# Two transformer layers in one kernel: the second attention's weights, first projections and constant rows moved into the experts' last batch

## The chip, the core and the metric

The kernel runs on one core of a Trainium2 chip. A core has five engines with queues of their own: PE (TensorE, matrix products into PSUM), ACT (ScalarE), DVE (VectorE), POOL (GpSimd) and SP (SyncE, which here issues nearly all DMAs). They are tied together by semaphores alone. The metric is the device time of one execution in microseconds (us), lower is better: 1503.14 us before the change, the median of three runs (1500.72 to 1504.99).

## The reference

Input `x` is 4 batches x 512 tokens x 256 features, all in float32. Two pre-norm layers:

```python
x = x + L0_attn(layernorm(x))   # 16 heads of 128, 8 kv heads, RMS norm, RoPE, window 128
x = x + L0_ffn(layernorm(x))    # 16 experts of 176, top 6 by softmax gate, and a shared one of 352
x = x + L1_attn(layernorm(x))   # below
x = x + L1_ffn(layernorm(x))    # ternary-quantized weights, 256 -> 1024 -> 256, exact gelu

def L1_attn(x):                 # 16 heads of 16
    q, k, v = (x @ W for W in (Wq, Wk, Wv))       # each split in heads
    p = softmax(q @ k.T * 0.25)
    return (p @ v) @ Wo + bo
```

## The kernel before

Nothing is tiled over cores; each layer part runs over the four batches, and a batch's 512 tokens are one tile of 512 columns. Products that need float32 precision are made of three passes in a faster format: every operand is split in a high and a low part (`_hi`, `_lo`), the high by a copy on ACT, the low by a subtraction on DVE or POOL, and `split_product` multiplies low x high, high x low, high x high. The order of the work on each engine is written out by hand, in functions of the same name for each engine: `attention_step` (first attention), `expert_step`, `pair_step` (second attention), `mlp_step`. Each step waits for semaphore counts that are worked out from the step's number. Middle batches run in hardware loops (`Fori`), the first and last are written out.

**Experts.** `expert_step(b, j, new, old)`: batch b, slice j of 25 slices of 128 hidden features. PE makes gate and up products of slice j (12 matmuls), ACT applies silu (L1168), DVE multiplies (L834), PE spreads the routing weight (`combine`, L1459), DVE multiplies by it (L844), ACT copies the high part (L1148), DVE subtracts the low (L850), and PE multiplies by the down weights (`down`, two steps behind). `new` says that there is a batch b in this step, `old` that batch b-1 still has work. After slice 24 come, with `b = 4` and `new` false, four steps in which only the last slices of batch 3 are finished, turned (L1447) and added to `x_res` (L818, semaphore `y_added`). The layer norm of the next layer part's first batch is made inside the last expert batch: `xnT` is ready in step 25.

**Between experts and second attention.** SP waits until all of `y_added` is there, then loads the second attention's weights (`wqk1`, `wv1`, `wo1`), a 1 MB tile of constants for `v1` (`c_vones`), the bias and the last layer's weights (2 MB). ACT and DVE split `wqk1`, PE projects tile 0 of q and of k (a tile is 8 heads of 16, 128 rows; `project_tile`), ACT and DVE split them into `qk1`.

**Second attention.** Heads of 16 rows are small for a 128-row array. So a head's q and k are stacked: high, high, low of q over high, low, high of k, 48 rows, and a row of ones in k beside the negated row maximum in q, 64 rows per head, two heads (a pair) in 128. The stacking changes partitions, and is done by DMA through a scratch tensor in DRAM: `keep_copies(b, tile)` writes six copies (L377), `stack_pair(b, n)` reads pair n back (L389) into rings of four, `qst` and `kst`. The constant rows of these rings are set once, on POOL and DVE (L506 to L508, L945). `pair_step(b, n, new, old)` is pair n of batch b, eight places i in it: scores for the maximum (L1583), reduced on DVE (L909), maxima turned (L1608) and added to q (`qsm`), scores again transposed (L1596), exponentials on ACT (L1223, tile pT), products with v (L1622, ring of two pairs), result copied by ACT (oT, L1255, at place i = 5 of each even pair), turned by PE (L1636, at i = 6) and divided on DVE. Spread over these places are the remaining projections: tile 1 of q at (n, i) = (0, 5), of k at (1, 3), the values in halves at (2, 5) and (3, 0), tile 0 of the next batch at (4, 5) and (5, 3), and the turns of the next batch's normed input. Their result goes through PSUM bank 0; ACT copies the high part and the raw value, POOL subtracts (`low_tile`, L525), `raw_kept` and `raw_used` count this.

SP issues its DMAs strictly in the order of its program. In batch b that is: copies of tile 0, pairs 0 to 3, copies of tile 1, pairs 4 to 7; `stack_pair` waits until the pair four before has been used, and at n = 0 and 4 until the copies have landed.

Of the kernel before, what the change touches and what calls it, by code (L numbers as in the profile page):

```python
# [13 lines left out]
F32 = mybir.dt.float32  # L14
# [7 lines left out]
P = 128  # L22
# [30 lines left out]
VW = 32  # L53
# [5 lines left out]
STACK_ROWS = 3 * HD1  # L59
STACKED = 2 * 2 * 16  # L60
# [3 lines left out]
RAW_USES, FIRST_USES, LAST_USES = 8, 6, 6  # L64
# [8 lines left out]
def build(nc, dram, out):  # L73
    with ExitStack() as ctx:
# [84 lines left out]

        wqk1 = [sb(f"wqk1_{part}", [P, KT, 2 * D], F32R, part_c) for part in ("hi", "lo")]  # L160
        wv1 = [sb(f"wv1_{part}", [P, KT, D], F32R, part_c) for part in ("hi", "lo")]

        vzero = sb("vzero", [P, STACK_RING * SEQ], where=part_c)
        pT1 = sb("pT1", [P, 2, 4, TT, SEQ], where=part_c)
        wo1 = sb("wo1", [P, KT, D], where=part_c)
        bo1 = sb("bo1", [P, D], where=part_c)
        stack = sb("stack", [P, 4], where=part_c)
        v1 = sb("v1", [P, TT, HEADS1 * VW], where=part_c)
        qk1 = [sb(f"qk1_{part}", [P, 2, 2, SEQ], F32R, part_c) for part in ("hi", "lo")]
        qst = sb("qst", [P, STACK_RING, SEQ], F32R, part_c)  # L170
        kst = sb("kst", [P, STACK_RING, SEQ], F32R, part_c)
        qsm = sb("qsm", [P, 2, SEQ], F32R, part_c)
        nm1 = sb("nm1", [P, 2, TT, P], where=part_c)

        early = pT1[:, 1].rearrange("p h c f -> p h (c f)")
        wqk1_in, wv1_in = early[:, 0, 0:KT * 2 * D], early[:, 1, 0:KT * D]
        oT1 = sb("oT1", [P, 2, SEQ], where=part_c)
        oinv = sb("oinv", [P, 2, TT, 4], where=part_c)
        otok = sb("otok", [P, TT, D], where=part_c)
        oTn = sb("oTn", [P, KT, SEQ], where=part_c)  # L180

        wm1 = sb("wm1", [P, KT, DFF], where=part_c)
        wm2 = sb("wm2", [P, HT, D], where=part_c)
        ones = sb("ones", [P, P], where=part_c)
# [1659 lines left out]
```

## Time and profile before

| | us |
|---|---|
| median of 3 runs | 1503.14 |
| profiled execution | 1504.41 |
| its span | 1502.7 |
| PE busy | 1395.5 (93%) |
| DVE busy | 1084.1 (72%) |
| ACT busy | 731.6 (49%) |
| POOL busy | 471.9 (31%) |

The first attention takes the span up to about 690 us, the experts up to 1089, the second attention up to about 1415, the last layer part the rest. The profile's mean granted clock of PE is 0.957 of full speed; full is 2.4 GHz, the other level, 1.2 GHz, shows as 0.50. In timelines the length of a matmul is that of one from issue to end; back to back they overlap.

### The profile page before, as it was taken

The numbers are of one execution on the slowest core, as the hardware profiler recorded it, in microseconds if no ns is written. First come the engines' busy times: TensorE is split into PE (matmuls) and PEld (weight loads), VectorE is DVE, ScalarE is ACT, GpSimd is POOL, SyncE is SP. The second block draws the span as 40 slices with busy tenths as digits, with TensorE's granted clock in tenths as the row PEclk, the third lists the DMA queues.
The fourth block names the chain that finished last, engine by engine and source line by source line (L and its number), as shares of the span: only waits on it lengthen the run. The fifth ranks groups of instructions, "written<-read, shape, count | busy, mean of one in ns | idle before, by whom it ended". The sixth has DMA issues, their size and how long they took to land.

```text
span 1502.7 us, 24489 instructions
## 1 busy us (share of the span) xinstructions
PE 1395.5 (93%) x7518; PEld 1058.9 (70%) x7518; DVE 1084.1 (72%) x2508; ACT 731.6 (49%) x1885; POOL 471.9 (31%) x727
## 2 busy tenths in 40 slices
PE   4799999999999998899999999999849899999898
PEld 3689889888998897677777777777624344444476
DVE  6999999899999995676555555455436776677454
ACT  4555565556556553444322322322216566666575
POOL 5766657666765663000000000000023031312110
PEclk9899999999999999899999999999957899999999
DMA  5200000000000000322000000000062222232001
GB/s 181 71 2 2 2 2 1 3 1 2 1 1 1 2 1 17 116 86 63 1 1 1 0 0 0 0 0 0 0 203 71 84 85 91 89 91 77 1 15 43
DMA packets 30941, 52.80 MB, mean 35 GB/s; under 512 B 4496, under 2 KB 12688, under 8 KB 30448
## 3 DMA queue, kind: packets, MB, share of 16 engines
q1 hardware_dynamic: 30432, 50.76, 10.9%
q8 instruction: 53, 0.87, 0.3%
q0 software_dynamic: 400, 0.71, 0.3%
q14 instruction: 56, 0.46, 0.1%
HBM read 37.49 MB, written 14.68 MB: 35 GB/s over the span
## 4 chain that ended last, share of the span: by engine, by line
PE 70%; DVE 13%; POOL 5%; issue 5%; ACT 4%; DMA 2%; SPq 1%; DVEq 0%; ACTq 0%; POOLq 0%
PE ps L1309 13%; PE ps L1311 13%; PE ps L1310 13%; PE ps L1583 5%; PE ps L1622 4%; PE ps L1395 4%; PE ps L1353 4%; POOL rope L462 2%; DVE qkn L705 2%; DVE ssum L716 2%; PE ps L1708 2%; POOL rms L460 2%; PE ps L1459 2%; PE ps L1381 1%; PE ps L1730 1%
## 5 line engine op out<-in xcount | busy, mean ns | idle before, releaser
L909 DVE TENSOR_REDUCE nm<-ps 128x1 f32<-128x512 f32 x256 | 166.2, 685 | 92.9 <-PE ps L1583 92.4
L1309 PE MATMUL ps<-xnT_lo,w1moe_hi 128*128 128x512 f32 x400 | 178.2, 445 | 2.0 <-DVE w2moe_lo L867 1.8
L1223 ACT ACTIVATE pT<-ps 128x512 f32<-128x512 f32 x256 | 142.5, 598 | 73.6 <-PE ps L1596 72.4
L1310 PE MATMUL ps<-xnT_hi,w1moe_lo 128*128 128x512 f32 x400 | 161.6, 404 | 0.0
L1311 PE MATMUL ps<-xnT_hi,w1moe_hi 128*128 128x512 f32 x400 | 160.5, 401 | 0.0
L421 POOL TENSOR_TENSOR ln_rs<-ln_ve,minus_half 128x4 f32<-128x4 f32 x12 | 13.6, 1131 | 466.3 <-DVE ln_ve L579 466.3
L1148 ACT ACTIVATE moe_act_hi<-sg 128x512 fp32r<-128x512 f32 x100 | 63.4, 634 | 190.3 <-DVE sg L844 190.3
L834 DVE TENSOR_TENSOR sg<-ps,sg 128x512 f32<-128x512 f32 x100 | 69.0, 690 | 97.4 <-ACT sg L1168 97.3
L462 POOL TENSOR_TENSOR rope<-rope 128x384 f32<-128x384 f32 x128 | 132.6, 1036 | 0.0
L1309 PE MATMUL ps<-wqkv_lo,xnT_hi 128*128 128x512 f32 x256 | 126.9, 496 | 6.1 <-issue 3.2
L1583 PE MATMUL ps<-kst,qst 64*128 64x512 f32 x256 | 106.9, 495 | 16.5 <-DMA kst<-copies 14.5
L1395 PE MATMUL ps<-qkT 128*128 128x128 f32 x896 | 121.9, 276 | 0.0
L680 DVE TENSOR_TENSOR yT<-yT,rsums 128x256 f32<-128x256 f32 x128 | 116.1, 907 | 3.2
L1596 PE MATMUL ps<-qsm,kst 64*128 64x512 f32 x256 | 110.9, 495 | 6.4 <-ACT pT L1223 6.4
L850 DVE TENSOR_TENSOR moe_act_lo<-sg,moe_act_hi 128x512 fp32r<-128x512 f32 x100 | 69.2, 692 | 65.4 <-ACT moe_act_hi L1148 65.3
L460 POOL TENSOR_TENSOR rms<-msq,minus_half 128x3 f32<-128x3 f32 x128 | 110.4, 863 | 10.0
L1108 ACT ACTIVATE yT<-ps,nmax 128x128 f32<-128x128 f32 x256 | 92.4, 373 | 39.6 <-DVE nmax L696 39.3
L1395 PEld LDWEIGHTS ps<-qkT 128*128 128x128 f32 x896 | 111.1, 193 | 0.5
L1168 ACT ACTIVATE sg<-ps 128x512 f32<-128x512 f32 x100 | 59.8, 598 | 101.6 <-PE ps L1311 101.5
L1583 PEld LDWEIGHTS ps<-kst,qst 64*128 64x128 f32 x256 | 45.1, 204 | 89.1 <-DVE nm L909 52.0
L1068 ACT ACTIVATE probT<-ps 128x256 f32<-128x256 f32 x128 | 49.2, 384 | 111.8 <-PE ps L1353 56.7
L1353 PE MATMUL ps<-parted,v 128*128 128x256 f32 x384 | 99.3, 381 | 3.8 <-POOL parted L448 1.9
(213 smaller groups left out, 3701.6 us busy)
## 6 DMA issues: line engine op xcount, KB each, us to landing
copies<-qk_hi SPq DMA_DIRECT2D x32, 256.0 KB
yT<-in_w1moe SPq DMA_DIRECT2D x25, 256.0 KB, 2.6
qst<-copies SPq DMA_DIRECT2D x64, 96.0 KB, 2.2
kst<-copies SPq DMA_DIRECT2D x64, 96.0 KB, 2.2
x_res<-in_wqkv SPq DMA_DIRECT2D x8, 512.0 KB, 4.8
copies<-qk_lo SPq DMA_DIRECT2D x16, 256.0 KB
w_in<-in_w2moe SPq DMA_DIRECT2D x25, 128.0 KB, 2.7
x_res<-in_wo SPq DMA_DIRECT2D x4, 512.0 KB, 3.9
```

Of the source, the lines that this page charges most:

```text
L460: nc.gpsimd.tensor_tensor(rms[:, s, :], msq[:, s, :], minus_half[:, 0:3], ALU.pow).then_inc(rms_ready, 1)
L462: nc.gpsimd.tensor_tensor(rope1[:, s, :], rope1[:, s, :], rope2[:, s, :], ALU.add).then_inc(rotated, 1)
L680: V.tensor_tensor(prob[:, m % PROB_RING], prob[:, m % PROB_RING], rsums[:, s, :].unsqueeze(2).to_broadcast((P, 2, P)), ALU.mult).then_inc( ...
L909: V.tensor_reduce(nm1[:, n % 2, t, col:col + 1], ps[:, 1 + s1_slot(p), :], AX.X, ALU.max, negate=True).then_inc(s1_max, 1)
L1223: A(pT1[:, u % 2, 2 * (m % 2) + h, c, :], ps[:, 4 + e % 2, :], ACT.Exp, scale=SCALE1).then_inc(p1_ready, 1)
L1309: MM(out, left[0], right[1], start=first, stop=False)
L1310: MM(out, left[1], right[0], start=False, stop=False)
L1311: return MM(out, left[0], right[0], start=False, stop=last)
L1353: ins = MM(ps[:, 6, 0:2 * P], v0[:, (m if part else m - GROUPS) % V_RING, :], parted[:, r, part].rearrange("p h f -> p (h f)"), start=part ...
L1395: ins = MM(bank[:, h, part, :], qkT[:, m % K_RING, h, :], qkT[:, (m if part else m - GROUPS) % K_RING, 2, :], start=not alone(m) and h == ...
L1583: MM(ps[:, 1 + s1_slot(p), :], qst[rows, n % STACK_RING, t * P:(t + 1) * P], kst[rows, n % STACK_RING, :], start=True, stop=True).then_inc ...
L1596: MM(ps[:, 4 + e % 2, :], kst[rows, m % STACK_RING, c * P:(c + 1) * P], qsm[rows, m % 2, :], start=True, stop=True).then_inc(st_ready, 1)
```

## The change

- The weights of the second attention are loaded when slice 12 of the experts' last batch is through (`gu_ready` 88), those of the last layer part from slice 20 on, no longer after the experts. For that the SBUF tiles are laid out anew, over expert weights that are no longer needed; the incoming weights have tiles of their own.
- ACT splits `wqk1` behind step 16 and `wv1` behind step 17 of the experts' last batch, DVE behind steps 17 and 18. For that ACT and DVE run the last batch written out instead of in the loop.
- On PE, both tiles of q and k and the values of batch 0 are projected among the four closing expert steps, into PSUM banks 0 to 3, 0 and 6. ACT and DVE split them from there; in `pair_step` the projections of batch 0 at (0, 5), (1, 3), (2, 5), (3, 0) go.
- The scratch in DRAM has 64 rows per head, with the 16 constant rows written once at the start (two DMAs of 0.5 MB from `c_rows`), and no batch dimension: `keep_copies` waits for the reads of the batch before. A pair is loaded by two DMAs of 128 rows instead of four of 48. The constant settings of `qst` and `kst` go. `v1` and `nm1` are set by POOL memsets inside the experts, instead of a 1 MB load.
- In batch 0 the copies of tile 1 are issued after pair 0's loads, before pair 1's.
- ACT's copy oT is at i = 4 instead of 5.
- `wneg` has one buffer instead of two.

```diff
-STACK_ROWS = 3 * HD1
-STACKED = 2 * 2 * 16
+STACK_ROWS, HEAD_ROWS = 3 * HD1, 64
+STACKED = 2 * 16
 KEPT_COPIES = 2 * 3 * 16
...
-RAW_USES, FIRST_USES, LAST_USES = 8, 6, 6
+RAW_USES, FIRST_USES, LAST_USES = 8, 4, 6
...
+            for which in range(2):
+                sp.dma_start(copies[:, which, :, STACK_ROWS:HEAD_ROWS, :],
+                             dram["c_rows"][which].unsqueeze(0).unsqueeze(0).to_broadcast(
+                                 (2, HEADS_T, HEAD_ROWS - STACK_ROWS, SEQ))).then_inc(rows_kept, 16)
...
-            wait(sp, y_added, BATCHES * TT)
-            sp.dma_start(wqk1_in, dram["wqk1"]).then_inc(wqk1_loaded, 16)
-            sp.dma_start(stack[:], dram["c_stack"]).then_inc(c_rest_loaded, 16)
-            sp.dma_start(wv1_in, dram["wv1"]).then_inc(wv1_loaded, 16)
-            for name, dst in (("wo1", wo1), ("c_vones", v1)):
-                sp.dma_start(dst[:], dram[name]).then_inc(c_rest_loaded, 16)
+            sp.wait_ge(gu_ready, (BATCHES - 1) * FT + 13)
+            sp.dma_start(wqk1_in[:], dram["wqk1"]).then_inc(wqk1_loaded, 16)
+            sp.dma_start(wv1_in[:], dram["wv1"]).then_inc(wv1_loaded, 16)
+            sp.dma_start(wo1[:], dram["wo1"]).then_inc(c_rest_loaded, 16)
             sp.dma_start(bo1[:], dram["bo1"].unsqueeze(0).to_broadcast((P, D))).then_inc(c_rest_loaded, 16)
+            sp.wait_ge(gu_ready, (BATCHES - 1) * FT + 21)
             for name, dst in (("wm1", wm1), ("wm2", wm2), ("b1m", b1m), ("b2m", b2m)):
                 sp.dma_start(dst[:], dram[name]).then_inc(wd_loaded, 16)
+            sp.wait_ge(rows_kept, 2 * 16)
 
             def keep_copies(b, tile):
...
+                if b >= 1:
+                    for s in range(STACK_RING):
+                        sp.wait_ge(stacked[s], STACKED * (2 * (b - 1) + tile + 1))
                 for which in range(2):
-                    if b == 0 and tile == 0:
-                        sp.wait_ge(qk1_split, which + 1)
+                    if b == 0:
+                        sp.wait_ge(qk1_split, 2 * tile + which + 1)
                     else:
                         sp.wait_ge(raw_used, (raw_before(b) if tile else raw_before(b - 1) + 4) + which + 1)
                     for copy, part in enumerate(COPIES[which]):
-                        sp.dma_start(copies[b, tile, which, :, copy * HD1:(copy + 1) * HD1, :],
...
-                    for h in range(2):
-                        sp.dma_start(dst[64 * h:64 * h + STACK_ROWS, n % STACK_RING, :].bitcast(F32),
-                                     copies[b, n // PAIRS_T, which, n % PAIRS_T * 2 + h]
-                                     ).then_inc(stacked[n % STACK_RING], 16)
+                    h = n % PAIRS_T * 2
+                    sp.dma_start(dst[:, n % STACK_RING, :].bitcast(F32),
+                                 copies[n // PAIRS_T, which, h:h + 2].rearrange("h r f -> (h r) f")
+                                 ).then_inc(stacked[n % STACK_RING], 16)
...
-                if b == 0:
-                    sp.wait_ge(c_consts_ready, 3)
                 for n in range(PAIRS):
-                    if n == PAIRS_T:
+                    if n == (1 if b == 0 else PAIRS_T):
                         keep_copies(b, 1)
...
+            pool.wait_ge(gu_ready, (BATCHES - 1) * FT + 13)
+            nc.gpsimd.memset(nm1[:], 0.0).then_inc(c_consts_ready, 1)
+            nc.gpsimd.memset(v1[:], 0.0).then_inc(c_consts_ready, 1)
+            pool.wait_ge(c_consts_ready, 2)
+            nc.gpsimd.memset(v1[:].rearrange("p t (h c) -> p t h c", h=HEADS1)[:, :, :, HD1:HD1 + 1], 1.0
+                             ).then_inc(c_consts_ready, 1)
             pool.wait_ge(y_added, BATCHES * TT)
-            nc.gpsimd.memset(vzero[:], 0.0).then_inc(zero_set, 1)
-            nc.gpsimd.memset(nm1[:], 0.0).then_inc(c_consts_ready, 1)
-            nc.gpsimd.memset(qst[:].bitcast(F32), 0.0).then_inc(c_consts_ready, 1)
-            pool.wait_ge(c_rest_loaded, 4 * 16)
...
+                expert_step(0, j, True, False, True)
+            with dve.Fori(1, BATCHES - 1) as b:
                 for j in range(FT + 1):
                     expert_step(b, j, True, True)
-            for j in range(4):
-                expert_step(BATCHES, j, False, True)
-            dve.wait_ge(y_added, BATCHES * TT)
-
...
+            for j in range(FT + 1):
+                expert_step(BATCHES - 1, j, True, True)
+                if j == 17:
+                    split_weights(1, wqk1, wqk1_in)
+                if j == 18:
+                    split_weights(2, wv1, wv1_in)
+            expert_step(BATCHES, 0, False, True)
+            expert_step(BATCHES, 1, False, True)
+            split_tile(0, 0, 0, 0)
+            split_tile(0, 0, 1, 1)
+            expert_step(BATCHES, 2, False, True)
+            split_tile(0, 1, 0, 2)
+            split_tile(0, 1, 1, 3)
+            expert_step(BATCHES, 3, False, True)
...
-            split_tile(0, 0, 0, 0)
-            split_tile(0, 0, 1, 1)
-            dve.wait_ge(zero_set, 1)
-            dve.wait_ge(c_rest_loaded, 4 * 16)
-            V.tensor_scalar(kst[:].rearrange("p r f -> p (r f)"), vzero[:], stack[:, 0:1], None, ALU.add
-                            ).then_inc(c_consts_ready, 1)
-            split_weights(2, wv1, wv1_in)
...
+            for j in range(FT + 1):
+                expert_step(BATCHES - 1, j, True, True)
+                if j == 16:
+                    split_weights(wqk1_loaded, wqk1, wqk1_in)
+                if j == 17:
+                    split_weights(wv1_loaded, wv1, wv1_in)
+            expert_step(BATCHES, 0, False, True)
+            split_tile(0, 0, 0, 0, False)
+            split_tile(0, 0, 1, 1, False)
+            expert_step(BATCHES, 1, False, True)
+            split_tile(0, 1, 0, 2, False)
+            split_tile(0, 1, 1, 3, False)
+            act.wait_ge(c_consts_ready, 3)
...
-                    if new and (n, i) in ((0, 5), (1, 3)):
+                    if new and old and (n, i) in ((0, 5), (1, 3)):
...
-                    if n % 2 == 0 and i == 5 and valid((n - 4) // 2):
+                    if n % 2 == 0 and i == 4 and valid((n - 4) // 2):
...
-            for j in range(4):
-                expert_step(BATCHES, j, False, True)
-            pe.wait_ge(y_added, BATCHES * TT)
...
-                    if new and (n, i) == (0, 5):
-                        if old:
-                            pe.wait_ge(raw_kept, before)
-                        else:
-                            pe.wait_ge(qk1_split, 2)
+                    if new and old and (n, i) == (0, 5):
...
-            for which in range(2):
-                project_tile(0, 0, which, which)
+            project_tile(0, 0, 0, 0)
+            project_tile(0, 0, 1, 1)
+            expert_step(BATCHES, 0, False, True)
+            project_tile(0, 1, 0, 2)
+            expert_step(BATCHES, 1, False, True)
+            project_tile(0, 1, 1, 3)
+            expert_step(BATCHES, 2, False, True)
+            pe.wait_ge(qk1_split, 1)
+            pe.wait_ge(wc_split, 2)
+            project_values(0, 0, 0)
+            expert_step(BATCHES, 3, False, True)
+            project_values(0, 1, 6)
+            pe.wait_ge(qk1_split, 4)
...
-    dram["copies"] = nc.dram_tensor("copies", (BATCHES, 2, 2, P // HD1, STACK_ROWS, SEQ), F32, kind="Internal").ap()
+    dram["copies"] = nc.dram_tensor("copies", (2, 2, HEADS_T, HEAD_ROWS, SEQ), F32, kind="Internal").ap()
...
```

Three places of the order. PE at the end of the experts, before: the down products of the last two slices (`moe_act`), the turns of the result (L1447), then the first projection (`wqk`).

```order
L1309 MATMUL ps<-moe_act_lo,w2moe_hi 128x512
L1310 MATMUL ps<-moe_act_hi,w2moe_lo 128x512
L1311 MATMUL ps<-moe_act_hi,w2moe_hi 128x512
L1447 MATMUL ps<-ident,yT 128x128 [waits yT_ready]
L1447 MATMUL ps<-ident,yT 128x128 x3
L1447 MATMUL ps<-ident,yT 128x128 [waits y_added]
L1447 MATMUL ps<-ident,yT 128x128 x3
L1309 MATMUL ps<-xnT_lo,wqk_hi 128x512 [waits wc_split,xnT_ready,y_added]
```

After, on PE at the same place, from the end of the second projection on (`cpieces` is the combine):

```order
L1334 MATMUL ps<-xnT_hi,wqk_hi 128x512
L1482 MATMUL ps<-cpieces,sel 128x512 [waits weighted]
L1332 MATMUL ps<-moe_act_lo,w2moe_hi 128x512 [waits act_ready]
L1333 MATMUL ps<-moe_act_hi,w2moe_lo 128x512
L1334 MATMUL ps<-moe_act_hi,w2moe_hi 128x512
L1332 MATMUL ps<-moe_act_lo,w2moe_hi 128x512
L1333 MATMUL ps<-moe_act_hi,w2moe_lo 128x512
L1334 MATMUL ps<-moe_act_hi,w2moe_hi 128x512
L1332 MATMUL ps<-xnT_lo,wqk_hi 128x512
```

The first two projections stand before the last combine, the next ones between the down products; the first of all no longer waits for `y_added`.

SP at the start of the second attention, before: weights, six copies of tile 0, then loads of pairs.

```order
L367 DMA b2m<-in_b2m 128x2
L377 DMA copies<-qk_hi 8x16x512 [waits qk1_split]
L377 DMA copies<-qk_hi 8x16x512
L377 DMA copies<-qk_lo 8x16x512
L377 DMA copies<-qk_hi 8x16x512 [waits qk1_split]
L377 DMA copies<-qk_lo 8x16x512
L377 DMA copies<-qk_hi 8x16x512
L389 DMA qst<-copies 48x512 [waits copies_kept0,c_consts_ready]
L389 DMA qst<-copies 48x512
```

After, from pair 0's loads on:

```order
L398 DMA qst<-copies 128x512 [waits copies_kept0]
L398 DMA kst<-copies 128x512
L386 DMA copies<-qk_hi 8x16x512 [waits qk1_split]
L386 DMA copies<-qk_hi 8x16x512
L386 DMA copies<-qk_lo 8x16x512
L386 DMA copies<-qk_hi 8x16x512 [waits qk1_split]
L386 DMA copies<-qk_lo 8x16x512
L386 DMA copies<-qk_hi 8x16x512
L398 DMA qst<-copies 128x512
L398 DMA kst<-copies 128x512
```

Between the loads of pair 0 and of pair 1 there are now the six copies of tile 1.

ACT around pair 4 of batch 0, before: exponentials (pT), evictions of a projection (qk_hi, raw), then oT.

```order
L1223 ACTIVATE pT<-ps 128x512 [waits st_ready] x5
L1194 ACTIVATE qk_hi<-ps 128x512 [waits qk1_ready,copies_kept0]
L1209 ACTIVATE raw<-ps 128x512 [waits raw_used]
L1255 ACTIVATE oT<-ps 128x512 [waits o1_ready]
L1223 ACTIVATE pT<-ps 128x512 [waits st_ready] x6
```

After, at the same place:

```order
L1249 ACTIVATE pT<-ps 128x512 [waits st_ready] x4
L1281 ACTIVATE oT<-ps 128x512 [waits o1_ready]
L1249 ACTIVATE pT<-ps 128x512 [waits st_ready]
L1206 ACTIVATE qk_hi<-ps 128x512 [waits qk1_ready,copies_kept0]
L1235 ACTIVATE raw<-ps 128x512 [waits raw_used]
L1249 ACTIVATE pT<-ps 128x512 [waits st_ready] x6
```

oT stands one exponential and two evictions earlier.

## Rows read from the trace of the kernel before

**Rows 1.** The chain of waits, 1080 to 1230 us: start, length, what.

```profile
1089.31 3.62 DMA pT<-in_wqk
...
1101.42 0.70 DVE qk_lo L893
...
1103.66 7.99 DMA copies<-qk_hi
...
1113.06 2.18 DMA kst<-copies
1115.29 3.56 PE ps L1583 x6
```

**Rows 2.** Timeline of PE, 1070 to 1156 us: start, length, line, tiles, idle before.

```profile
1075.77 0.39 PE L1309 MATMUL ps<-moe_act_lo,w2moe_hi 128*128 128x512 f32 x1
...
1081.48 0.50 PE L1309 MATMUL ps<-moe_act_lo,w2moe_hi 128*128 128x512 f32 x1 [1.32 <-DVE moe_act_lo L850]
...
1123.21 0.79 PE L1583 MATMUL ps<-kst,qst 64*128 64x512 f32 x1 [0.35 <-DVE nm L909]
...
1126.13 0.79 PE L1309 MATMUL ps<-xnT_lo,wqk_hi 128*128 128x512 f32 x1
...
1128.98 0.79 PE L1583 MATMUL ps<-kst,qst 64*128 64x512 f32 x1
...
1151.32 0.50 PE L1583 MATMUL ps<-kst,qst 64*128 64x512 f32 x1
```

**Rows 3.** Timeline of DVE, 1070 to 1120 us.

```profile
1074.63 0.69 DVE L850 TENSOR_TENSOR moe_act_lo<-sg,moe_act_hi 128x512 fp32r<-128x512 f32 x1 [0.70 <-ACT moe_act_hi L1148]
...
1077.67 0.69 DVE L844 TENSOR_TENSOR sg<-ps,sg 128x512 f32<-128x512 f32 x1 [0.37 <-PE ps L1459]
1079.55 1.29 DVE L594 TENSOR_TENSOR xnT_lo<-ps,xnT_hi 128x512 fp32r<-128x512 f32 x2 [1.18 <-ACT xnT_hi L1034]
```

**Rows 4.** Timeline of ACT, 1070 to 1085 us.

```profile
1073.96 0.64 ACT L1148 ACTIVATE moe_act_hi<-sg 128x512 fp32r<-128x512 f32 x1 [1.82 <-DVE sg L844]
```

**Rows 5.** Busy time by window: PE, PEld, DVE, ACT, POOL, clock, DMA share, GB/s.

```profile
1090.00:1104.00 14.00, 5.28 (x12) 3.79 (x12) 4.50 (x6) 2.77 (x4) 6.15 (x4) 0.63 0.95 322
1104.00:1111.00 7.00, 0.00 (x0) 0.00 (x0) 0.04 (x1) 0.00 (x0) 0.00 (x0) 0.50 0.52 203
1130.00:1131.00 1.00, 0.63 (x3) 0.00 (x0) 1.00 (x2) 0.98 (x2) 0.75 (x1) 0.50 0.33 121
1135.00:1140.00 5.00, 5.00 (x18) 3.36 (x19) 4.01 (x7) 2.70 (x6) 4.80 (x5) 0.50 0.38 128
1145.00:1150.00 5.00, 4.66 (x30) 2.37 (x28) 4.27 (x7) 3.65 (x8) 0.00 (x0) 1.00 0.28 80
1165.00:1170.00 5.00, 5.00 (x20) 2.51 (x22) 2.06 (x4) 2.67 (x6) 1.07 (x1) 0.63 0.47 124
```

**Rows 6.** Timeline of the SP queue, 1080 to 1130 us: DMA issues.

```profile
1099.76 1.34 SPq L377 DMA_DIRECT2D copies<-qk_hi  x2
...
1124.26 1.22 SPq L377 DMA_DIRECT2D copies<-qk_hi  x2
```

**Rows 7.** Waits of PE, 1115 to 1500 us: total, times, longest.

```profile
PE ps L1583 <- DMA kst<-copies: 14.5, 1, 14.5
PE ps L1636 <- ACT oT L1255: 14.2, 16, 1.3
```

**Rows 8.** Timeline of all engines, 1156 to 1170 us.

```profile
1158.44 0.60 ACT L1194 ACTIVATE qk_hi<-ps 128x512 fp32r<-128x512 f32 x1 [0.78 <-PE ps L1311]
...
1159.41 0.60 ACT L1255 ACTIVATE oT<-ps 128x512 f32<-128x512 f32 x1
...
1160.07 0.66 PE L1636 MATMUL ps<-ident,oT 128*128 128x128 f32 x4 [1.29 <-ACT oT L1255]
...
1168.78 1.07 PE L1622 MATMUL ps<-pT,v 128*32 128x512 f32 x8
```

**Rows 9.** Timeline of PE, 1180 to 1192 us.

```profile
1185.33 1.93 PE L1622 MATMUL ps<-pT,v 128*32 128x512 f32 x8
```

More of the change, by code:

```diff
@@ L376, in keep_copies @@
                     for copy, part in enumerate(COPIES[which]):
-                        sp.dma_start(copies[b, tile, which, :, copy * HD1:(copy + 1) * HD1, :],
+                        sp.dma_start(copies[tile, which, :, copy * HD1:(copy + 1) * HD1, :],
                                      qk1[part][:, tile, which, :].bitcast(F32)).then_inc(copies_kept[tile], 16)
@@ L538, in _ @@
                 i = b + BATCHES + 1
-                for which in range(2):
-                    low_tile(b, which, b, 1, which)
+                if b >= 1:
+                    for which in range(2):
+                        low_tile(b, which, b, 1, which)
                 rstd(i)
@@ L819, in add_half, with expert_step @@
                                     ALU.add).then_inc(y_added, 1)
-            def expert_step(b, j, new, old):
-                if new and isinstance(b, int) and j + 2 < FT:
+            def expert_step(b, j, new, old, first=False):
+                if first and j + 2 < FT:
                     split_moe(j + 2)
@@ L1131, in split_moe, with expert_step @@
                 A(w2moe[0][:, j, :], w2_in[:, j % 2, :], ACT.Copy).then_inc(moe_high, 1)
-            def expert_step(b, j, new, old):
-                if new and isinstance(b, int) and j + 2 < FT:
+            def expert_step(b, j, new, old, first=False):
+                if first and j + 2 < FT:
                     split_moe(j + 2)
@@ L1449, in turn_half, with expert_step @@
                 ins.then_inc(y_turned, 1)
-            def expert_step(b, j, new, old):
+            def expert_step(b, j, new, old, first=False):
                 k = b * FT + j
@@ L1488, in expert_step @@
                 if new and j < FT:
-                    if isinstance(b, int):
+                    if first:
                         pe.wait_ge(moe_split, j + 1)
@@ L1689, in _ @@
             pe.wait_ge(wc_split, 1)
-            for which in range(2):
-                project_tile(0, 0, which, which)
+            project_tile(0, 0, 0, 0)
[11 more added lines that the diff above has]
+            pe.wait_ge(qk1_split, 4)
             for n in range(PAIRS):
```

112 lines of the change are left out of this document (53 added, 59 removed).

## The prediction

> **What bounds the kernel now.** I read the page first: TensorE (PE) is busy in most slices of the span, and the one deep hole lies between the experts and the second attention. Then the chain of waits over that hole [rows 1]: after the last expert output is added (1089.3 us) the chain is a weight load (3.62 us), its split, the first projections, their split (ends 1102.1), the copies of q and k to DRAM (7.99 us), one load back (2.18 us), and only at 1115.29 the first score matmul. PE alone says the same: one wait of 14.5 us, "DMA kst<-copies" [rows 7]. Third, windows over the hole: clock 0.50, DMA share first 0.95 at 322 GB/s, then 0.52 at 203 GB/s with no engine at work [rows 5]. Last, the waits of PE behind the hole: the largest left is 16 waits, 14.2 us in all, for ScalarE's copy oT [rows 7].
>
> **The end of the experts.** PE's last expert matmuls are held by a short ring (combine, DVE multiply, ACT copy, DVE subtract), with a 1.32 us gap before one down product [rows 2]. The change puts two projections ahead of the last combine and two more between the down products. xnT is split at 1079.55 + 1.29 = 1080.84 [rows 3]. A projection took 2.85 us at 1.2 GHz (1126.13 to 1128.98 [rows 2]), so about 1.42 at 2.4 GHz, the clock here. Two end at 1083.7. Then combine (one matmul, 0.4), DVE 0.69, ACT 0.64 and DVE 0.69 for the last expert slice [rows 3, 4]: 1086.1 to 1086.3; behind it on DVE the first q subtract (0.70 [rows 1]): 1087.0, k's 1087.7. Before, k's ended at 1102.1. PE meanwhile has two down products, two projections and two halves of the values, each as many columns as a projection (1.42), and two turns of 0.66: 1083.7 + 0.4 + 6 x 1.42 + 1.3 = 1093.9. What is late next is not PE but the copies.
>
> **The copies.** They go at 203 GB/s when nothing else runs [rows 5]. Three of them, first issued at 1124.26, had landed by 1131 [rows 5, 6]: 0.79 MB at 203 GB/s is 3.9 us, so issue and landing add 2.8. Six are 1.57 MB: 7.7 + 2.8 = 10.5 us from the first issue. Issued at 1087.1 they land at 1097.6. Before, it was 11.9 us from the first issue at 1099.76 [rows 6] to 1103.66 + 7.99 = 1111.65 [rows 1]: 4.3 MB of weights and constants (by their shapes) were still in the queue. Now two issues load a pair instead of four: 0.9 us of issue and 2.18 us of landing [rows 1], less a little, 2.8 us. First score matmul at 1100.4 instead of 1115.3: **-14.9 us**. Bounds: -17 if the copies overlap their issue better, -12 if the larger loads (128 rows instead of 48) land a microsecond or two later.
>
> **The second pair.** On SP's queue the six copies of tile 1 now stand between the loads of pair 0 and those of pair 1. Whatever stands behind them waits: in 1090 to 1104 the queue moved 14.0 x 322 = 4.5 MB, the 4.3 MB of weights that stood first, and in 1104 to 1111 7.0 x 203 = 1.4 MB, about the whole of the copies issued from 1099.8 on [rows 5]. So the queue served them in order. Copies issued from 1098.5 land at 1109.0; pair 1 starts at 1110.5. Pair 0 itself has eight score matmuls, six in 3.56 us [rows 1], to 1105.2: PE waits 5 us, at 1.2 GHz. Before, pair 1 began at 1123.21 [rows 2], 7.9 us behind pair 0; now 10.1 behind: **+2.2 us**. Bounds: -2.8 (pair 1 is there when pair 0 ends) to +4.
> The Trainium skill says of this (DMA: Bandwidth & Descriptors, section "Queues, rings and completion order") that on each engine descriptors are consumed in ring order. By that rule pair 1 can't pass the copies on the engines which both use; the rows agree as far as they go. Without it pair 1 would start near 1105.5 and the sum be 5 us lower.
>
> **Pairs 1 to 3 of batch 0.** 1123.21 to 1151.32 is 28.1 us [rows 2]. Out go one projection (2.85), one half of the values at 1.2 GHz (2.85, as many columns) and one at 2.4 GHz (1.4): 7.1 us, all PE time with no cover (PE busy 5.00 of 5.00 in 1135 to 1140 [rows 5]). Against that, before, the clock rose from 0.50 (1135 to 1140) to 1.00 (1145 to 1150 [rows 5]) in the course of the values; with PE idle until 1110 and thin work behind, pair 3 may run at 1.2 GHz. I price it at 1.3: **-5.8 us**. Bounds -7.1 and -1.
>
> **Steady pairs.** ACT's copy oT moves one exponential ahead, before the projection's evictions too. In the rows: oT runs from 1159.41, and PE's turn starts at 1160.07 after 1.29 us of idle [rows 8]. ACT idles while PE projects (0.78 us before the eviction at 1158.44 [rows 8]), so the copy fits there, and the work behind it comes earlier. The later exponentials come no later. 15 of 16 waits can go (the last, at the very end, waits for PE's own result): at most 14.2 - 0.7 = 13.5. Zero is the other end (an exponential becomes late instead, by the same 0.5 us). I take **-11 us**, near the waits' row since the idle is read on the engine that is busy around it.
> Four stretches at 1.2 GHz in batches 0 to 2 begin just behind such a wait (the first holds 1165 to 1170, clock 0.63 [rows 5]). A projection in one costs 1.4 more, eight matmuls with v 1.93 instead of 1.07 [rows 8, 9]; about 3 us a stretch. If the denser PE keeps its clock in one or two: **-3 us**. Bounds +6 (two new stretches) and -10.
>
> **Small parts.** Weights split inside batch 3: 1024 columns cost at most twice a 512-column copy or subtract, 1.28 on ACT, where the gap is 1.82 [rows 4], and 1.38 on DVE, where it is 0.37 [rows 3]. So the multiply there is 1.0 late; the subtract behind it ended at 1074.63 + 0.69 = 1075.32 and was needed at 1075.77 [rows 2, 3], slack 0.45. **+0.5 us** once; the values' split is half as long and nearly fits. Bounds 0 and 1.5. The 4.3 MB of loads run beside 30 us or more of experts, the memsets on an idle POOL, the constant rows behind the input load where SP has nothing to do until the first attention ends: 0. The ternary weights now share one buffer, written and read by DVE in order: 0. The new SP waits for `stacked` name loads of a batch earlier: 0. Loads per pair grow from 0.39 to 0.52 MB, but in steady pairs PE waited for none [rows 7]: 0; if that cover fails, 1 us a pair.
>
> **Sum.** -14.9 + 2.2 - 5.8 - 11 - 3 + 0.5 = -32.0. The profiled execution took 1504.41 us (span 1502.7 and 1.7 around it), 1.3 above the median of 1503.14. That gives 1472.4 against it and 1471.1 against the median; I say 1472.
>
> **The rivals.**
> A, forecast: all terms about as priced, 1472, its own range 1464 to 1481.
> B, the early copy of oT only moves the wait to the next exponential. For it: ACT has eight exponentials of some 0.6 us a pair and PE's transposed scores follow them by two. Against: ACT is idle just ahead of the eviction [rows 8]. Then -11 and -3 fall away: 1486.
> C, PE keeps 2.4 GHz more than I think (no dips in batches 0 to 2, pair 1 not behind the copies): -32 - 5 - 7: 1460.
> D, slower than before: the clock doesn't come back. The change takes out of pairs 1 to 3 the dense projections and values behind which the clock rose in the rows (0.50 to 1140, 1.00 from 1145 [rows 5]), and leaves 6 to 7 us of idle in front. Eight matmuls with v cost 1.93 instead of 1.07 [rows 8, 9], and scores and turns stretch alike. PE is busy 4.66 of 5 us at full clock too [rows 5], so most of it comes on top: 6 us for a pair of 9.4 (28.1 for three). To eat 32 us it needs 5.5 pairs more at 1.2 GHz than I count; through batches 0 and 1 (12 pairs) it would be +72 - 32 = +40: 1543. Against it: the clock was back at 1.00 by 1145 [rows 5], and a stretch like 1165 to 1170 is over before eight matmuls with v at 1168.78 take 1.07 [rows 8].
> The Trainium skill (TensorE: Matmul & The Clock Gate, "What's actually happening") holds the slow clock to be the default, which activity releases; by that the thinned pairs are at risk: the rows put them at 1472, the rule taken strictly puts them on D's side. No row shows such thin pairs.
> E, the moved work does not shorten anything, since the copies are hidden or late anyway: 14.5 us of PE's wait end with them, so only if they started no earlier; 1503.
>
> **How the numbers follow.** A 0.55, B 0.22, C 0.15, D 0.04, E 0.02, others 0.02. The range takes A's with B's and most of C's: 1458 to 1489. Measurement tells about 0.3% (4.5 us) from no change. Faster: A, B, C: 0.93. Same: E and part of the rest, 0.03. Slower: D and a half-failed clock, 0.04.
>
> **What would show it.** In the profile after: first projections at 1080.9, no gap of 1.3 us before the down product; copies issued near 1087 and the first score matmul at 1100; a PE wait of some 6 us for pair 0's load, and a second of some 5 us for pair 1's; pair 4 of batch 0 near 1133; the 14.2 us for oT down to 1 or 2; clock 0.50 from about 1096 to pair 3. Wrong if pair 1 waits for nothing, if oT's waits come back as waits for pT of like size, or if the clock stays at 0.50 beyond pair 4.

## The result, and the profile after

The changed kernel takes 1467.95 us (median of 4 runs, 1465.12 to 1470.54), the kernel before, on the same chip, 1504.07 (4 runs, 1500.72 to 1506.41): ratio 0.9761, 95% interval 0.9730 to 0.9793, so 36 us are gone. Line numbers have moved: L1601 is now the first scores (before L1583), L1614 the transposed ones (L1596), L1640 the products with v (L1622), L1654 the turn of oT (L1636), L1281 the copy oT (L1255), L386 and L398 the copies and the loads from scratch.

The chain of waits over the hole, start, length, what; it answers to [rows 1]:

```profile
1078.51 1.30 DVE xnT_lo L605 x2
1079.85 0.50 PE ps L1332
...
1085.34 0.61 DVE qk_lo L900
...
1086.04 0.66 SPq L386
...
1090.90 6.43 DMA copies<-qk_hi
...
1105.83 6.62 DMA kst<-copies
1112.50 1.22 PE ps L1601 x2
```

The weight load is no longer in it. The first projection follows the split of xnT at once, q's low part is ready at 1085.95 instead of 1102.12, and the chain then runs through copies, SP's issues and one load. This profiled execution was 1.04 us early before anything that the change touches (xnT_lo at 1078.51, before 1079.55 [rows 3]); this is taken off below.

PE's timeline of the second attention's first pairs (x8 and x2: matmuls; in brackets the idle before), beside [rows 2]:

```profile
1100.94 4.73 PE L1601 MATMUL ps<-kst,qst 64*128 64x512 f32 x8 [8.51 <-DMA kst<-copies]
1112.50 1.22 PE L1601 MATMUL ps<-kst,qst 64*128 64x512 f32 x2 [6.83 <-DMA kst<-copies]
...
1131.61 1.94 PE L1640 MATMUL ps<-pT,v 128*32 128x512 f32 x8
...
1137.56 0.50 PE L1601 MATMUL ps<-kst,qst 64*128 64x512 f32 x1
```

There are two waits for DMA, one for pair 0 and a new one for pair 1, 11.56 us behind it; pair 4 starts at 1137.56 instead of 1151.32. SP's queue shows what pair 1 waited for:

```profile
1098.21 1.21 SPq L386 DMA_DIRECT2D copies<-qk_hi  x2
1099.46 0.77 SPq L386 DMA_DIRECT2D copies<-qk_lo  x1
1100.28 1.45 SPq L386 DMA_DIRECT2D copies<-qk_hi  x1
1101.78 1.56 SPq L386 DMA_DIRECT2D copies<-qk_lo  x1
1103.38 1.20 SPq L386 DMA_DIRECT2D copies<-qk_hi  x1
1104.62 1.18 SPq L398 DMA_DIRECT2D qst<-copies  x1
1105.83 1.08 SPq L398 DMA_DIRECT2D kst<-copies  x1
```

Tile 1's six copies occupy SP for 6.4 us, and the load behind them lands 6.6 us after its issue, against a median of about 3 for such a load.

PE's waits from 1080 us on (total, times, longest) and the steady part around one oT, beside [rows 7, 8]:

```profile
PE ps L1601 <- DMA kst<-copies: 15.3, 2, 8.5
PE ps L1614 <- ACT pT L1249: 3.2, 11, 0.5
...
PE ps L1654 <- ACT oT L1281: 0.7, 1, 0.7
```

```profile
1158.96 0.59 ACT L1281 ACTIVATE oT<-ps 128x512 f32<-128x512 f32 x1
...
1159.61 0.66 PE L1654 MATMUL ps<-ident,oT 128*128 128x128 f32 x4
```

The wait for oT has gone from 14.2 us to 0.7, and the turn starts 0.06 us after the copy with no idle in front. It has not come back as a wait for pT. Windows (columns as in [rows 5]; after first, then the kernel before from its own pair 4 on):

```profile
1096.00:1101.00 5.00, 0.06 (x1) 0.09 (x1) 0.00 (x0) 0.00 (x0) 0.00 (x0) 0.53 0.48 150
1101.00:1112.00 11.00, 4.67 (x8) 2.16 (x8) 4.88 (x8) 0.00 (x0) 0.00 (x0) 0.50 0.74 248
1112.00:1137.00 25.00, 23.78 (x76) 11.43 (x76) 18.94 (x38) 13.23 (x23) 8.73 (x7) 0.50 0.16 54
...
1140.00:1145.00 5.00, 5.00 (x33) 2.03 (x25) 2.99 (x5) 3.24 (x7) 1.17 (x1) 1.00 0.35 105
1137.00:1463.70 326.70, 307.40 (x1726) 165.36 (x1718) 227.95 (x423) 218.10 (x391) 62.14 (x48) 0.98 0.24 78
1165.00:1170.00 5.00, 5.00 (x18) 1.73 (x18) 3.41 (x6) 1.77 (x3) 0.00 (x0) 0.50 0.33 105
```

```profile
1151.00:1502.70 351.70, 318.34 (x1722) 171.13 (x1718) 228.37 (x424) 218.95 (x393) 62.44 (x48) 0.94 0.20 63
```

All of pairs 1 to 3 ran at 1.2 GHz, and the clock was back just behind them. The second thing to see is in the two long windows: the same work (1722 matmuls before, 1726 after) kept PE busy for 318.3 us before and 307.4 after, and left it idle for 33.4 and 19.3. So of 25 us that went here 14 were idle and 11 were work that ran faster: nobody took work from PE, but its clock was 0.98 instead of 0.94.

### The profile page after: what moved, and what is told of

Its sections match the earlier page's. It is cut to its first block, busy times and chain, and to the rows that moved or that the text cites. A ratio compares the mean times of both kernels' runs of the same rounds, so it can differ in the third digit from the quotient of the medians.

```text
span 1463.7 us, 24351 instructions
## 1 busy us (share of the span) xinstructions
PE 1379.4 (94%) x7518; PEld 1048.3 (72%) x7518; DVE 1083.8 (74%) x2509; ACT 730.2 (50%) x1883; POOL 469.0 (32%) x725
## 4 chain that ended last, share of the span: by engine, by line
PE 68%; DVE 15%; POOL 5%; issue 5%; ACT 2%; DMA 2%; SPq 1%; DVEq 0%; ACTq 0%; POOLq 0%
PE ps L1332 13%; PE ps L1334 12%; PE ps L1333 12%; PE ps L1601 5%; PE ps L1640 5%; PE ps L1418 4%; PE ps L1376 3%; DVE ssum L727 2%; DVE qkn L716 2%; POOL rope L469 2%; PE ps L1732 2%; POOL rms L467 2%; PE ps L1482 2%; DVE nmax L707 2%; PE ps L1754 1%
## 5 line engine op out<-in xcount | busy, mean ns | idle before, releaser
L1601 PE MATMUL ps<-kst,qst 64*128 64x512 f32 x256 | 107.5, 494 | 17.1 <-DMA kst<-copies 15.3
L1614 PE MATMUL ps<-qsm,kst 64*128 64x512 f32 x256 | 111.9, 491 | 3.4 <-ACT pT L1249 3.2
L1601 PEld LDWEIGHTS ps<-kst,qst 64*128 64x128 f32 x256 | 44.7, 200 | 88.3 <-DVE nm L930 53.5
L1097 ACT ACTIVATE rope<-ps 128x384 f32<-128x384 f32 x128 | 62.8, 491 | 81.7 <-PE ps L1334 81.4
```

Source lines behind the costliest of these rows:

```text
L1601: MM(ps[:, 1 + s1_slot(p), :], qst[rows, n % STACK_RING, t * P:(t + 1) * P], kst[rows, n % STACK_RING, :], start=True, stop=True).then_inc ...
L1614: MM(ps[:, 4 + e % 2, :], kst[rows, m % STACK_RING, c * P:(c + 1) * P], qsm[rows, m % 2, :], start=True, stop=True).then_inc(st_ready, 1)
```

## The experiments

**Two kernels that separate the copy oT from the rest.** One is the kernel before with oT one place earlier, the other the changed kernel with oT back at its old place:

```diff
 # kernel before
-                    if n % 2 == 0 and i == 5 and valid((n - 4) // 2):
+                    if n % 2 == 0 and i == 4 and valid((n - 4) // 2):
 # changed kernel
-                    if n % 2 == 0 and i == 4 and valid((n - 4) // 2):
+                    if n % 2 == 0 and i == 5 and valid((n - 4) // 2):
```

> The kernel before with one edit: ACT's copy oT at i = 4. Theory one (waits only): the 16 waits of PE for oT, 14.2 us, shrink to 1 or 2, the stretches at 1.2 GHz stay: about 1491. Theory two (waits and clock): the stretches at 1.2 GHz in batches 0 to 2 that begin behind such waits go too, 11 to 12 us more: about 1479, and the granted clock from 1151 us to 1410 is 0.97 or more, not 0.93. Rival (the wait moves to the next exponential): 1502 to 1505, waits for pT up by as much.

> The changed kernel with ACT's copy oT back at i = 5. Waits only: 1468 + 13 = 1481. Waits and clock: 1468 + 25 = 1493, with stretches at 0.50 near (4, 5) of batches 0 to 2. Rival (the place of the copy is worth nothing): 1468.

Measured, in one session with the kernel before at 1504.91: 1480.63 (ratio 0.9835, 0.9815 to 0.9856) and 1490.61 (0.9906, 0.9887 to 0.9926). PE's waits of the second kernel, which has everything of the change but this:

```profile
PE ps L1654 <- ACT oT L1281: 14.2, 16, 1.3
PE ps L1614 <- ACT pT L1249: 4.7, 17, 0.5
```

So the copy alone is worth 24 us in the kernel before, and taking it out of the changed one costs 23. The rest is worth 14 (1504.9 to 1490.6) or 13 (1480.6 to 1468.0). The two ratios multiply to 0.9743, beside 0.9761 for both together: the parts add up, and none hides the other. The traces put the copy's share where it was expected: from the first matmul of batch 0's pair 4 to the end the kernel before takes 351.4 us (from 1151.32), the changed kernel with oT late 352.0 (from 1136.72), the changed kernel 326.1. But the waits for oT were 14.2 us. Where do the other 10 come from?

**Filling the wait instead of removing it.** The kernel before, with four unused matmuls on PE ahead of the wait for oT, in 14 of the 16 turns (`if new` leaves out the last two; the trace has 56 of these matmuls, where the expectation below says 15 turns); their result is read by nobody:

```diff
-                        pe.wait_ge(oT1_kept, kq + u + 1)
                         if valid(n - 1):
                             pe.wait_ge(qsm_ready, kb + n)
                         else:
                             pe.wait_ge(o1_normed, kq + u)
+                        for m in range(4 if new else 0):
+                            MM(ps[:, 7, :], wqk1[0][:, 0, 0:P], wqk1[0][:, 0, :], start=True, stop=True)
+                        pe.wait_ge(oT1_kept, kq + u + 1)
```

> The kernel before, with four unused matmuls of 512 columns (about 0.24 us each, as the 34 unused ones of an earlier run that took 8.10 us) on PE ahead of the wait for oT, in every steady pair (15 of 16 turns); nobody reads their result. So the wait is not shortened, only filled. Theory (the idle of 0.9 to 1.3 us before the turn is what brings the stretches at 1.2 GHz): the waits for oT fall to near 0, the time that they cost stays (filled), and the clock over 1150:1430 rises from 0.93 to 0.97 or more; only the clock's share comes back: 1504 - 10 = 1494, between 1490 and 1498. Rival 1 (the stretches come from the work in these places, not from the idle): the clock stays near 0.93, time 1504 to 1508. Rival 2 (PE is the bound and the matmuls do not fit the gap at 1.2 GHz): slower, 1508 to 1515.

Measured: 1495.34 (5 runs, 1494.20 to 1500.89), the kernel before 1503.79; ratio 0.9939, 0.9925 to 0.9952. Adding some 13 us of useless work (56 x 0.24) to the bounding engine made the kernel 8.5 us faster. Waits and window in its profile (an execution of 1500.9 us, the slowest of the five):

```profile
PE ps L1596 <- ACT pT L1223: 6.1, 17, 1.7
...
PE ps L1638 <- ACT oT L1255: 1.7, 4, 0.8
```

```profile
1151.00:1410.00 259.00, 248.52 (x1446) 118.35 (x1442) 187.81 (x329) 167.80 (x313) 55.84 (x43) 0.98 0.25 78
...
1165.00:1170.00 5.00, 4.73 (x28) 2.24 (x27) 4.50 (x8) 3.43 (x8) 0.41 (x1) 1.00 0.28 83
```

The same window in the kernel before:

```profile
1151.00:1410.00 259.00, 237.38 (x1349) 111.73 (x1345) 181.72 (x323) 164.17 (x307) 55.67 (x43) 0.93 0.25 77
```

The same 259 us have clock 0.93 in the kernel before, 0.92 in the changed kernel with oT late, 0.98 in the changed kernel, and 0.98 here. In the kernel before with oT early it is 0.95, below the 0.97 that was expected; that profile is of the slowest of its six executions (mean clock 0.960, the other five 0.966 to 0.970). Over whole executions, all nine of the kernel before that were measured beside it have a mean clock of 0.956 to 0.960, all five filled ones 0.965 to 0.971. The stretch 1165 to 1170, at 0.63 before [rows 5], is at 1.00.

The first rival of the expectation (the stretches belong to the work there and not to the idle, 1504 to 1508) is out, and so is the second: filling the idle in front of the turn took away the stretches at 1.2 GHz behind it. But the idle isn't enough by itself. In the kernel before it lasts 1.24 to 1.30 us ahead of six turns and at most 0.81 ahead of the others. Stretches of some 8 us begin behind four of the six long ones (1160.07 [rows 8], 1197.70, 1235.26, 1306.59), none behind the other two (1271.33, 1342.82), and none behind the shorter ones up to 1400 us:

```profile
1271.33 0.66 PE L1636 MATMUL ps<-ident,oT 128*128 128x128 f32 x4 [1.24 <-ACT oT L1255]
```

```profile
1237.00:1243.00 6.00, 5.94 (x17) 3.46 (x17) 3.76 (x8) 2.21 (x6) 0.00 (x0) 0.50 0.23 66
1272.00:1278.00 6.00, 5.46 (x32) 2.79 (x32) 5.53 (x13) 3.95 (x8) 0.15 (x2) 1.00 0.20 63
1308.00:1314.00 6.00, 5.58 (x16) 3.22 (x15) 4.09 (x8) 2.51 (x5) 0.00 (x0) 0.55 0.20 55
1344.00:1350.00 6.00, 5.47 (x32) 2.54 (x30) 5.97 (x13) 4.43 (x9) 0.53 (x1) 1.00 0.24 68
```

A fifth stretch (1182 to 1190) stands behind a wait of 1.6 us for DVE, which is busy with a long reduction (wabs, 2.3 us); it comes back in the filled kernel (1186 to 1190) and in the changed one (1164 to 1172). Stretches also begin where PE has had no wait above 0.3 us, as from 1358 us on in the kernel before with oT early. What decides between these places isn't shown.

The account of the copy oT is then: waits 13.5, clock 8.5, together 22, beside the 23 to 24 measured. The 8.5 is a net figure: 13.3 us of fill and 1.7 us of waits left are 0.8 more than the 14.2 us of waits that they replace, so the clock's share is an estimated 9.3.

**Tile 1's copies at their old place in SP's queue.**

```diff
-                    if n == (1 if b == 0 else PAIRS_T):
+                    if n == PAIRS_T:
                         keep_copies(b, 1)
```

> The changed kernel with batch 0's copies of tile 1 issued before pair 4's loads, as in the other batches, not before pair 1's. Theory (pair 1's loads stand behind six copies in the queue): PE's second wait of 6.8 us for kst goes, pair 1 starts 5.5 us after pair 0 instead of 11.6, and 5 to 6 us of it stay: 1462 to 1463. Rival one (pair 1's loads are late by themselves, two sets of 0.25 MB): the wait stays above 3 us, 1466 to 1468. Rival two (given back at pair 4, whose copies come later): 1468, with a wait for kst at pair 4.

Measured: 1462.01 (1458.08 to 1463.33), ratio 0.9717, 0.9695 to 0.9739. PE's timeline:

```profile
1102.13 5.92 PE L1601 MATMUL ps<-kst,qst 64*128 64x512 f32 x10 [8.31 <-DMA kst<-copies]
...
1125.94 1.65 PE L1640 MATMUL ps<-pT,v 128*32 128x512 f32 x8
```

Ten score matmuls in a row: pair 1 waits for no DMA, and pair 4, whose copies now come later, doesn't either (the 8.31 us is PE's only wait for kst). Both rivals are out. The first products with v come 46.0 us behind xnT_lo (1079.90 in this execution) instead of 53.1, 7 us earlier, and the medians differ by 6. The intervals of the two ratios overlap a little (0.9739 and 0.9730), the single runs don't (at most 1463.33 here, at least 1465.12 in the changed kernel). So putting these copies early, which the change did, cost 6 us by itself: they held the loads of a pair that was needed at once, for one that is needed 25 us later.

**The first projections behind the experts' end.** The changed kernel with all four `expert_step` ahead of the projections and their splits on PE, ACT and DVE; weights are loaded and split early as before:

```diff
-            project_tile(0, 0, 0, 0)
-            project_tile(0, 0, 1, 1)
-            expert_step(BATCHES, 0, False, True)
...
+            for j in range(4):
+                expert_step(BATCHES, j, False, True)
+            project_tile(0, 0, 0, 0)
+            project_tile(0, 0, 1, 1)
```

> The changed kernel with all projections of batch 0 behind the four closing expert steps, on PE, ACT and DVE; the weights are loaded and split early as before. Theory (the early place of the first two projections starts the copies earlier): first copy issued 5 us later, 1473. Rival (only the early loads count, and the copies' start is hidden): 1467 to 1469.

Measured: 1472.92 (1471.40 to 1473.29), ratio 0.9789, 0.9769 to 0.9808; 5 us above the changed kernel in the median. The intervals of the ratios overlap (0.9769 and 0.9793), the single runs don't (at least 1471.40 here, at most 1470.54 there). The trace agrees: the first copy is issued at 1091.23, 11.8 us behind xnT_lo (1079.38) instead of 7.5, and pair 0 starts 26.7 us behind it instead of 22.4. So of the 13.3 us by which pair 0 moved, 4.3 belong to the place of the projections; the other 9 are left for the early weights and for fewer, larger loads, which weren't run apart.

**PE kept at work through the copies.** The kernel with tile 1's copies late, and 34 unused matmuls ahead of pair 0, read by nobody:

```diff
             pe.wait_ge(qk1_split, 4)
+            for m in range(34):
+                MM(ps[:, 5, :], wqk1[0][:, 0, 0:P], xnT[0][:, 0, :], start=True, stop=True)
```

> The kernel of e3 (batch 0's tile 1 copied late) with 34 matmuls of 512 columns, whose result nobody reads, put on PE where it waits 8.3 us for pair 0's load (34 x 0.234 = 8.0 us). Theory one (the stretch at 1.2 GHz in pairs 1 to 3 costs what PE's matmuls cost more): the clock stays at 1.00 up to pair 0 and beyond, pairs 0 to 3 take 3 to 5 us less, 1457 to 1459. Rival (pairs 0 to 3 are held by DVE's eight reduces and ACT's eight exponentials a pair, or the clock falls in pair 0 all the same): 1461 to 1463.

Measured: 1461.93 (5 runs, 1461.40 to 1463.18), ratio 0.9726, 0.9701 to 0.9751: the same as without them. Windows, and PE and DVE in the timeline of all engines:

```profile
1100.00:1105.00 5.00, 3.94 (x11) 1.50 (x9) 3.59 (x6) 0.00 (x0) 0.00 (x0) 1.00 0.91 293
1105.00:1110.00 5.00, 4.63 (x14) 2.36 (x13) 4.86 (x11) 0.76 (x1) 0.00 (x0) 0.57 0.56 215
1110.00:1120.00 10.00, 9.42 (x29) 5.00 (x28) 9.70 (x23) 7.04 (x13) 5.85 (x5) 0.50 0.32 120
```

```profile
1101.41 6.07 DVE L930 TENSOR_REDUCE nm<-ps 128x1 f32<-128x512 f32 x10 [9.28 <-PE ps L1601]
...
1102.16 2.89 PE L1601 MATMUL ps<-kst,qst 64*128 64x512 f32 x5 [0.32 <-DVE nm L930]
...
1105.24 1.30 PE L1601 MATMUL ps<-kst,qst 64*128 64x512 f32 x2 [0.19 <-DVE nm L930]
```

PE was at 2.4 GHz when pair 0 came, had gaps of 0.2 to 0.3 us behind DVE's reductions (0.61 each, back to back, 4.86 of 5.00 us busy), and fell to 1.2 GHz for pairs 1 to 3 all the same. While PE is fast DVE is the bound of pair 0: its score matmuls start every 0.6 us (five in 2.89), at DVE's pace. So the idle ahead of pair 0 isn't what slows the pairs behind it. What pairs 1 to 3 would take at 2.4 GHz this run doesn't show, since they never ran at it. It also isn't the case of the filled wait above: there PE had work on both sides of one gap, here the work itself is thin. That the gaps behind DVE are what lets the clock fall is argued from these rows, and was not tested apart.

**The scratch rows in another order.** In the changed kernel a copy writes rows `copy * 16` to `copy * 16 + 15` of each of 8 heads. With the rows ordered (row, copy) it writes every fourth row, 128 evenly spaced ones. First together with tile 1's copies late, then with 18 unused matmuls too, then alone:

```diff
-                        sp.dma_start(copies[tile, which, :, copy * HD1:(copy + 1) * HD1, :],
+                        sp.dma_start(copies[tile, which].rearrange("h (r c) f -> c (h r) f", c=4)[copy],
```

The constant rows are laid out to match (four DMAs instead of two, and `MAX_ROW` 3 instead of 48).

> The kernel of e3 with the rows of a head in the scratch ordered (row, copy) instead of (copy, row), the row of ones moved with them, so that a copy's target is 128 evenly spaced rows and not 8 x 16. Theory (a copy with an outer dimension of 8 is served by half of the DMA engines, 0.52 of them at 200 GB/s): the share rises above 0.8, six copies land 7 to 8 us after the first issue instead of 11.2, pair 0 starts 3 to 4 us earlier, 1458 to 1459. Rival (the copies' rate is that of small writes into DRAM, or of the issue on SP): share and times as before, 1462.

> e6 with 18 such matmuls (4.2 us) on PE ahead of pair 0. If both theories hold: 1454 to 1456. If only that of the DMA engines: as e6. If only that of the clock: as e5, or later by what the 18 matmuls overhang.

> The changed kernel, with tile 1's copies where it has them (behind pair 0's loads in batch 0), and only the order of the scratch rows changed to (row, copy), so that a copy writes 128 evenly spaced rows. If the layout acts as in the run that had both edits: six copies in 7.4 us instead of 10.9 from first to last, so pair 0 starts 3 to 3.5 us earlier (1097.5), and the next six hold pair 1's loads some 3 to 4 us less: pair 1 near 1106.5 instead of 1112.5. Then the two edits overlap: 1468 - 5.5 = 1462.5, between 1460 and 1464.5, and the late tile adds about 3 more on top (1458.9). Rival (SP's issue of about 1.4 us each, not the engines' share, held the copies): pair 0 gains at most 1 us, 1466 to 1468.

| kernel | us | ratio, interval |
|---|---|---|
| rows interleaved, tile 1 late | 1458.88 (1454.00 to 1460.17) | 0.9691, 0.9663 to 0.9719 |
| the same, 18 unused matmuls | 1457.61 (1457.30 to 1459.54) | 0.9700, 0.9675 to 0.9725 |
| rows interleaved alone | 1459.11 (1456.78 to 1462.19) | 0.9702, 0.9687 to 0.9718 |

The DMA activity of the same 11 us (1086 to 1097) in the changed kernel, then with the rows interleaved alone (tenths of 16 engines and GB/s, in 40 slices):

```profile
DMA  0000175243648554556553545555455555545321
GB/s 0 0 0 0 37 89 37 22 60 119 209 171 283 171 149 156 194 201 201 149 141 141 201 156 216 201 201 194 186 223 194 201 209 201 209 186 216 119 97 37
```

```profile
DMA  0000000000089999999999999951010000000097
GB/s 0 0 0 0 0 0 0 0 0 0 0 313 380 387 387 350 335 276 365 380 298 387 395 365 380 454 201 67 0 15 7 15 22 0 0 0 0 0 216 164
```

And SP's queue with the rows interleaved alone:

```profile
1088.22 0.81 SPq L387 DMA_DIRECT2D copies<-qk_hi  x2
...
1090.67 0.64 SPq L387 DMA_DIRECT2D copies<-qk_hi  x1
1095.53 0.32 SPq L399 DMA_DIRECT2D qst<-copies  x1
```

The same bytes go at some 370 GB/s instead of 200, with a share of 0.9 or more of the 16 DMA engines' time instead of 0.5, and from the first issue to the first load it takes 7.3 us (1088.22 to 1095.53) instead of 11.3 (1086.04 to 1097.35). SP is free sooner as well: the last three copies of tile 0 hold it 0.45 to 0.64 us each where they held it 1.4 to 1.7. The Trainium skill (DMA: Bandwidth & Descriptors, section "Why a DMA increments its semaphore by 16 and not by 1") has the rule: a DMA runs on the largest number of engines up to 16 that divides the slowest dimension (of a size above 1) of both of its sides. By it 8 heads give 8 engines and 128 rows 16. The trace agrees in the share, 0.5 and 0.9 or more; which engines worked it doesn't show. The rival of the first expectation, that small writes into DRAM set the rate, is out: these 11 us hold 816 packets in 43.0% of 16 engines' time, and 915 in 45.8% with the rows interleaved, some 90 ns a packet in both.

Alone, the layout is worth 8.8 us on top of the change, more than expected (1462.5): pair 0 comes 18.6 us behind xnT_lo (1080.71 there) instead of 22.4, and pair 1 25.4 us behind it instead of 34.0. With it, the early or late place of tile 1's copies no longer shows in the time (1459.11 and 1458.88). In the traces a part of it is left: with the early place PE still waits 2.1 us for pair 1, and the first products with v come 44.5 us behind xnT_lo, with the late place 42.3. But that second execution has more stretches at 1.2 GHz later on (clock 0.95 over 1151 to 1410, 0.98 in the first). So the two edits cure the same delay for the most part, and 2 us are within the spread of the runs. The run with 18 unused matmuls is as the one without, as expected if only the theory of the DMA engines holds: PE's clock was 1.00 up to 1100 us, and 0.63 and 0.50 in the 10 us behind. The three kernels can't be told apart, and all are 9 to 10 us below the changed one. The one with the layout alone is the smallest edit.

## Why the prediction was right, point by point

The forecast was 1472 with a range of 1458 to 1489, and A was the likeliest case; 1468 came, by A's mechanisms. But the sum was right in part because two errors cancelled: the hole was priced at 18 us (-14.9 + 2.2 - 5.8 + 0.5) and gave 13 to 14 (12.7 in the trace), the steady pairs at 14 and gave 23 to 24. That these errors had opposite signs is luck.

One reading of the prediction has to be set right first. It took 1123.21 for the start of pair 1 in the kernel before, but that is pair 1's second matmul. Pair 0 has eight score matmuls: six from 1115.29 on, and behind the projection two more, the first two of this row:

```profile
1121.64 1.22 PE L1583 MATMUL ps<-kst,qst 64*128 64x512 f32 x3
```

The third of the row is pair 1's first; a timeline from 1122.5 us on shows it alone:

```profile
1122.23 0.62 PE L1583 MATMUL ps<-kst,qst 64*128 64x512 f32 x1
```

So pair 1 began 6.9 us behind pair 0 and not 7.9. This moves 1.0 us from the third term to the second and leaves their sum as it is.

- **Pair 0, -14.9:** pair 0 started 14.35 us earlier, 1.04 of them this execution's early base, so -13.3. The first copy went out at 1086.04, and issue and landing took 11.3 us where the prediction had 10.5; the load behind took 3.6 from its issue to the first matmul (1097.35 to 1100.94), where it had 2.8. The mechanism was right, inside the bounds of -17 and -12.
- **Pair 1, +2.2:** +4.6 (11.56 us behind pair 0, before 6.9), a little outside the bounds (-2.8 to +4). SP's queue served the copies first, as read, but SP itself was held longer by each of these issues (6.4 us for six), and the load behind them landed only 6.6 us after its issue. Late copies removed the wait, which shows the cause.
- **Pairs 1 to 3, -5.8:** -4.0 (25.06 us where it was 29.1 by the same correction). The removed work was read rightly as 7.1 us; by subtraction the clock took back 3.1 of it, where 1.3 was put in. All 25 us ran at 1.2 GHz, where the prediction had taken it to be back in pair 3. This is the mild form of rival D, whose severe form (batches 0 and 1 slow) didn't come: the clock was 1.00 from 1140 on. A part of this term is chance: with the same code up to there, the kernels before with oT early and with the filled wait took 31.0 us for pairs 1 to 3 and the one before 29.1, and the changed kernel with oT late took 23.4 and the changed one 25.1, each by when the clock came back.
- **oT, -11:** -13.5, the whole wait, so the upper bound. That oT's wait would move to the next exponential (rival B) is out: waits for pT are 3.2 us, and 4.5 in the kernel before with this edit alone.
- **Clock stretches, -3:** this is the term that failed in size. The filled wait measures about -8.5 for it, inside the bounds (+6 to -10). The prediction named the place (stretches begin just behind such a wait) and its price of 3 us a stretch, and then let only one or two of four go, since nothing in the rows said whether the idle was the cause or only stood beside it. All four went. From batch 0's pair 4 on, the changed kernel has two short stretches left in batches 0 to 3, one near 1165, where DVE's reduction of 2.3 us (wabs) makes PE wait 1.6 us for the next maximum, and one near 1372.
- **Small parts, +0.5:** 0. The experts' steps are 4.43 us in the split steps too, and PE's only wait of some size between 950 and 1076 us is one of 1.3 us, as before; the slack that the prediction saw was enough.

The signs named to look for came: projections at once (1079.85), copies near 1087 (1086.04), two DMA waits of 8.5 and 6.8 us where 6 and 5 were named, oT at 0.7. Pair 4 near 1133 was off: 1137.56, by the first three terms above.

## What to carry over

A short wait on the bounding engine can cost more than its length, by the clock behind it (here behind four of sixteen such waits); price it with the granted clock of the stretch that follows, and test it by filling the wait, which separates wait from clock. Before a transfer is moved ahead in a queue, look up which nearer load it will stand in front of. Where a DMA's share sits at a fraction like one half with nothing else at work, look at its outer dimension before moving it.

## What had not been expected of the hardware

- Useless work made the kernel faster: 56 unused matmuls (about 13 us of PE) gave 8.5 us back. The chip gave 2.4 GHz through four places where stretches at 1.2 GHz had followed an idle of 1.24 to 1.29 us.
- It isn't symmetric: 8 us of unused matmuls in front of the thin pairs didn't keep the clock in them (0.57 and 0.50 from 1105 on). That PE's gaps behind DVE's reductions are the reason is argued, not shown.
- With the shape of a DMA the time for which an issue holds the queue changed too: 1.4 to 1.7 us for copies at half the engines' share once some were outstanding, 0.45 to 0.64 us for the same bytes at the full share (tile 0's copies). Whether the shape itself or the longer backlog does this was not run apart; tile 1's copies, behind loads, held it up to 0.99 us at the full share.
- A load of 256 KB took a median of 3 us to land, but 6.6 us behind six such copies.
